# Layer 0's output product in one rounded pass over 96 rows, with GpSimd making a third of its operand

## The chip, the cores and the metric

The kernel runs on one core of a Trainium2 chip. The metric is device time in microseconds (us), the median of several runs. A core has five instruction streams that work beside each other and meet only through semaphores and DMA: TensorE (PE in the profile; its weight loads are PEld), VectorE (DVE), ScalarE (ACT), GpSimd (POOL) and SyncE (SP), which here only issues DMAs. Each executes its own list strictly in order.

## What is computed

128 entries of 64 rows, 256 wide, pass four conditioned residual layers, `x = x + layer(x)`:

```
# layer 0: a decoded low-rank map, K = 30
U = (mu @ W_dec + b_dec).reshape(B, 257, 30)
param = einsum('bik,kj->bij', U, V);  weight, bias = param[:, :-1], param[:, -1]
x = x + einsum('bsd,bde->bse', x, weight) + bias
# layer 1: demodulated linear map, clamped
y = einsum('blc,oc->blo', x * style, weight1) * dcoef
x = x + clip(y + bias1, -256, 256)
# layer 2: conditional adapter
x = x + relu(x @ (down*dg + db)) @ (up*ug + ub)
# layer 3: layer norms with gains looked up by class, then an MLP
h = ln(ln(x, pw_g[id], pw_b[id]), cp_g[c], cp_b[c]);  t = ln(x, tm_g[c], tm_b[c]);  s = ln(x, ms_g[m], ms_b[m])
x = x + ln(silu(cat([w0*h, w1*t, w2*(x+..), w3*(x+..), w4*(x+..), w5*s]) @ W1 + b1) @ W2 + b2, g, b)
```

Layer 0 is computed as t = U·x plus a bias part, 30 wide, and then x1 = x + t·V. The change is about t and t·V.

## The kernel before

The 8192 rows are 16 chunks of 512 rows, that is 8 entries each. Within a chunk TensorE does: t (L906: one bias product over 6 rows at L913, then 32 small u products at L919), x1 = t·V (L924, products at L935), l1 (layer 1, L948), dn and up (layer 2's adapter, L962 and L976), x3r and xht (transposes, L988 and L994), tm and ms (class gains of the t and s branches, L1008 and L1031), cp (class gains of h, L1035, products at L1046), hht (transposes of h, L994), and int_W1 in four parts whose names end in x3, tm, ms and h. int_W1 has its numbers split into high and low parts of the rounded float type fp32r, so each product is three, at L902, L903 and L904, of 128 rows by 512 columns.

x1's route through the engines is this. TensorE leaves t in PSUM in four strips of 32 rows. ScalarE's `act_th1` (th1, L1171) copies the four into rows 0 to 29 of `t_st`; its `act_th2` (th2, L1178) copies those to rows 32 to 61. `pe_x1` makes two fp32 products, one for each half of the features, each over its own 30 rows of `v_rep` and `t_st`. VectorE's `v_x1add` (L1345) adds x. GpSimd's `g_style` (style, L1516) multiplies by the style, and then l1 may run. So one chain goes th1, th2, x1, x1add, style, l1.

GpSimd also has, per chunk, hmul and hadd (L1546, L1551: h = xhat * gain + offset), wup (L1565, L1567: the adapter's weights), res (L1577), the gathers of table rows (L1507), and three small roots: rootx and rooth (L1523 to L1531, for the layer norms of x and h; their last result is nb_x or nb_h), and rooty (L1590, L1592, for the output's norm). rooty waits for ScalarE's squares y_sq (L1320) and is waited for by VectorE's y_out (L1486). ScalarE's normalisations of x and h stand at L1209 and wait for nb_x and nb_h.

The order of each queue is written out by hand as three lists (`run_slots`, L109): `begin`, then `order`, a list of (stage, lag) that a hardware loop repeats for iterations 6 to 15 (the stage works on chunk iteration minus lag), then `end`. So the steady part is ten iterations, and whatever stands ahead of iteration 6 or behind iteration 15 was placed by hand. Fillings (`pe_warm`, L537) are products of ones whose results nothing reads. `pads` is a list of tiles that are set to zero at the start, each element one more count of the semaphore `z_pad`.

Begin's setup part, up to the first chunk's x1, decodes U on TensorE (L487, 16 groups), builds tables and scales, and loads weights through SyncE's queue.

Of the kernel before, what the change touches and what calls it, by code (L numbers as in the profile page):

```python
# [122 lines left out]
def conditioned_residuals(nc, t):  # L123
    ctx = ExitStack()
    with ctx:
# [1683 lines left out]
```

## Time and profile before

| | us |
|---|---|
| runs (3) | 520.67, 521.92, 523.74; median 521.92 |
| profiled execution | 521.21 |
| its span on the chip | 519.4 |
| outside the span | 1.8 |

The profile is of one execution. Its page gives each engine's busy time, the busy share in 40 slices of the span, the chain that ended last, and groups of instructions by line. The trace behind it can be asked for single instructions: start, duration, the engine and line, tiles and shapes, and in brackets how long the engine stood idle before and what released it. Matmul ends are modelled and overlap, so the pace of TensorE is read from the starts. The mean granted TensorE clock was 0.994 of full speed.

### The profile page before, as it was taken

To read this page: it belongs to the slowest core of one execution; us is meant where nothing else is said; L and a number is where in the kernel's file an instruction comes from. 1 tells how busy PE (TensorE), PEld (TensorE's weight loads), DVE (VectorE), ACT (ScalarE), POOL (GpSimd) and SP (SyncE) were. 2 spreads that over 40 slices of the span, in tenths; PEclk is the share of its full clock that TensorE was granted. 3 is DMA by queue.
4 is the path that set the end of the run, shared out by engine and by line. 5 is a ranking of instruction groups with operands and counts; after the bars stand their busy time and mean duration, and the time that the engine had idled before them with its cause. 6 is when DMAs were issued, how large, how long until landed. Compare 5 with 4: busy or idle time off the path is not lost.

```text
span 519.4 us, 9425 instructions
## 1 busy us (share of the span) xinstructions
PE 486.3 (94%) x3198; PEld 354.2 (68%) x3198; DVE 405.8 (78%) x696; ACT 336.3 (65%) x638; POOL 391.0 (75%) x367
## 2 busy tenths in 40 slices
PE   2987887999999999999999999999999999998993
PEld 2953644767677776768686867677776768687682
DVE  2958876868788788888787878788787888886863
ACT  4573667456767676766777776767676767656832
POOL 6468799889878879697978787788779793787321
PEclk9999999999999999999999999999999999999997
DMA  8887705625252352608080716253442613104102
GB/s 299 247 304 208 203 20 124 163 73 135 83 127 81 77 171 56 191 24 223 0 229 17 205 43 173 74 136 112 106 142 63 175 47 90 49 21 145 40 2 81
DMA packets 34989, 61.78 MB, mean 119 GB/s; under 512 B 5017, under 2 KB 17413, under 8 KB 34580
## 3 DMA queue, kind: packets, MB, share of 16 engines
q1 hardware_dynamic: 28756, 43.98, 30.2%
q0 software_dynamic: 5344, 16.87, 11.3%
q10 hardware_dynamic: 864, 0.61, 0.4%
q8 instruction: 14, 0.23, 0.2%
q14 instruction: 11, 0.09, 0.1%
HBM read 52.58 MB, written 8.87 MB: 118 GB/s over the span
## 4 chain that ended last, share of the span: by engine, by line
PE 79%; POOL 6%; DVE 5%; DMA 4%; issue 3%; ACT 2%; SPq 0%; DVEq 0%; POOLq 0%; ACTq 0%
PE ps_c L902 11%; PE ps_c L904 11%; PE ps_c L903 10%; PE ps_d L948 9%; PE ps_d L962 5%; PE ps_a L976 5%; PE ps_b L902 3%; PE ps_b L903 3%; PE ps_b L904 3%; PE ps_b L935 2%; PE ps_a L988 2%; DMA set_wdec<-in_nets_rows 2%; PE ps_a L994 2%; PE ps_b L994 2%; DMA set_wdec<-in_W_dec 1%
## 5 line engine op out<-in xcount | busy, mean ns | idle before, releaser
L1507 POOL DMA_INDIRECT pw_rows<-in_pw,gidx x64 | 65.0, 1016 | 17.9 <-issue 17.4
L948 PE MATMUL ps_d<-xm_t,l_w 128*128 128x512 f32 x128 | 59.0, 603 | 2.2 <-POOL xm_t L1516 2.2
L1209 ACT ACTIVATE h<-h,nb_h,rstd_h 128x256 f32<-128x256 f32 x64 | 33.3, 591 | 33.1 <-POOL nb_h L1531 33.0
L1240 ACT ACTIVATE tm_t_h<-ps_a 128x1024 fp32r<-128x1024 f32 x16 | 16.4, 1026 | 45.6 <-DVE ps_a L1413 45.6
L1516 POOL TENSOR_TENSOR xm_t<-x_t,style 128x1024 f32<-128x1024 f32 x16 | 30.5, 1905 | 20.2 <-DVE x_t L1345 20.1
L948 PEld LDWEIGHTS ps_d<-xm_t,l_w 128*128 128x128 f32 x128 | 23.1, 190 | 26.8 <-issue 24.2
L1546 POOL TENSOR_TENSOR h<-xhat,pw_rows 128x1024 f32<-128x1024 f32 x16 | 38.0, 2378 | 4.1 <-ACT xhat L1209 4.1
L1565 POOL TENSOR_TENSOR w_up<-up_rep,ugub 128x1024 f32<-128x1024 f32 x16 | 38.0, 2372 | 2.2 <-issue 2.0
L1551 POOL TENSOR_TENSOR h<-h,pw_rows 128x1024 f32<-128x1024 f32 x16 | 38.3, 2394 | 1.3
L1567 POOL TENSOR_TENSOR w_up<-w_up,ugub 128x1024 f32<-128x1024 f32 x16 | 38.1, 2382 | 1.3
L902 PE MATMUL ps_b<-w_h,act_t_l 128*128 128x256 f32 x128 | 37.7, 294 | 0.4 <-DVE act_t_l L1450 0.4
L1577 POOL TENSOR_TENSOR x3be<-x,ln_gb 128x1024 f32<-128x1024 f32 x16 | 37.8, 2364 | 0.0
L1352 DVE TENSOR_TENSOR ps_d<-ps_d,dcoef 128x1024 f32<-128x1024 f32 x16 | 19.7, 1232 | 21.6 <-PE ps_d L948 21.6
L903 PE MATMUL ps_b<-w_l,act_t_h 128*128 128x256 f32 x128 | 36.1, 282 | 0.0
L904 PE MATMUL ps_b<-w_h,act_t_h 128*128 128x256 f32 x128 | 36.0, 281 | 0.0
L1209 ACT ACTIVATE xhat<-ps_a,nb_x,rstd_x 128x256 f32<-128x256 f32 x64 | 31.0, 564 | 6.7 <-POOL nb_x L1531 6.7
L962 PE MATMUL ps_d<-x_t,down_w 128*64 128x256 f32 x256 | 31.2, 385 | 3.0 <-DVE x_t L1367 3.0
L976 PEld LDWEIGHTS ps_a<-act_dn,w_up 128*128 128x128 f32 x256 | 30.5, 191 | 4.9 <-issue 2.6
L976 PE MATMUL ps_a<-act_dn,w_up 128*128 128x128 f32 x256 | 31.6, 277 | 2.2 <-ACT act_dn L1188 1.2
L1590 POOL TENSOR_TENSOR ve_y<-y_var,eps 128x4 f32<-128x4 f32 x15 | 3.0, 202 | 40.2 <-ACT y_sq L1320 40.2
L1418 DVE TENSOR_TENSOR ps_d<-ps_d,xh_t 128x1024 f32<-128x1024 f32 x16 | 19.7, 1231 | 17.4 <-PE ps_d L1031 17.4
L1320 ACT ACTIVATE y_sq<-ps_b 128x256 bf16<-128x256 f32 x64 | 23.7, 380 | 14.8 <-PE ps_b L904 14.8
(251 smaller groups left out, 1551.2 us busy)
## 6 DMA issues: line engine op xcount, KB each, us to landing
ugub<-ugub_scratch SPq DMA_DIRECT2D x32, 512.0 KB, 6.8
x_t<-in_x_t SPq DMA_DIRECT2D x16, 512.0 KB, 5.7
out<-y_out SPq DMA_DIRECT2D x15, 512.0 KB, 7.3
set_wdec<-in_W_dec SPq DMA_DIRECT2D x2, 1920.0 KB, 9.6
set_wdec<-in_int_W SPq DMA_DIRECT2D x1, 1536.0 KB, 9.8
set_wdec<-in_nets_rows SPq DMA_DIRECT2D x1, 1152.0 KB, 12.2
pw_rows<-in_pw,gidx POOLq DMA_INDIRECT x64, 3.7
set_wdec<-in_nets_W SPq DMA_DIRECT2D x1, 768.0 KB, 4.8
```

Source lines behind the costliest of these rows:

```text
L902: eng.matmul(out, wl, ah, start=first, stop=False)
L903: eng.matmul(out, wh, al, start=False, stop=False)
L904: return eng.matmul(out, wh, ah, start=False, stop=last)
L948: m = eng.matmul(ps_l1[:, o, :], l1_w[:, k, o * P:(o + 1) * P], xm_t[:, k, :], start=k == 0, stop=k == KB - 1)
L962: m = eng.matmul(ps_dn[e * HID:(e + 1) * HID, part * CT * S:(part + 1) * CT * S], down_w[:, k, part * HID:(part + 1) * HID], x[:, k, e], s ...
L976: m = eng.matmul(ps_up[:, k, j * P:(j + 1) * P], w_up[:, j, k * P:(k + 1) * P], act_dn[:, j, :, :], start=True, stop=True)
L1209: m = eng.activation(out[:, j, :], src[:, j, :], ACT.Identity, bias=nb[k][:, j:j + 1], scale=rstd[k][:, j:j + 1])
L1507: eng.indirect_dma_start(pw_rows[c.ring][:, j, :], None, t["pw"], bass.IndirectOffsetOnAxis(ap=gidx[c.ring][:, j:j + 1], axis=0)).then_inc ...
L1546: eng.tensor_tensor(h1[:, :, :], xhat[:, :, :], pw_rows[c.ring][:, :, 0:D], ALU.mult).then_inc(g_h1m, 1)
L1551: eng.tensor_tensor(h1[:, :, :], h1[:, :, :], pw_rows[c.ring][:, :, D:2 * D], ALU.add).then_inc(g_h1, 1)
L1565: eng.tensor_tensor(w_up[:, :, :], q, ugub[:, :, 0:D], ALU.mult).then_inc(g_upm, 1)
L1567: eng.tensor_tensor(w_up[:, :, :], w_up[:, :, :], ugub[:, :, D:2 * D], ALU.add).then_inc(g_up, 1)
```

## The change

- **x1 as one rounded product.** `t_st` becomes an fp32r tile of 96 rows: t's low part in rows 0 to 29, its high part in rows 32 to 61 and again in rows 64 to 93. `v_st`, made once, holds V's high part, its high part again, and its low part. x1 is then two products (one per half of the features) over all 96 rows.
- **t's route.** th1 writes t to an fp32 tile `t_f`, and waits for the low part of the chunk before. th2 copies `t_f` three times into `t_st` (three strips of 30 rows) and waits for x1 of the chunk before. A new stage on GpSimd, `g_tlow` (tlow, L1549 in the new file), writes t_f minus its high part into rows 0 to 29; it waits for th2. x1 waits for both. The two ScalarE semaphores become one that counts twice.
- **v_st.** `act_vhigh` on ScalarE (it waits for three weight loads, `up_rep` the last) and `v_vlow` on VectorE, once, in begin.
- **t's bias in strips.** One product of 6 rows by 128 columns becomes four of 128 rows by 32 columns; `ub_ch` and `entry_oh` are zeroed first.
- **cp in full rows.** The four cp products (24 rows each, in two row groups that ran in pairs) contract over all 128 rows; the gain table's unused rows are zeroed first.
- **Fillings.** `ones` is set first on GpSimd, and 22 products of ones stand ahead of the decoder. Six each follow x1(2), cp(0) and l1(2).
- **Tiles.** The class indices move to partitions 32 to 55 of the tile whose first rows are `t_f`.

```diff
-            wait(eng, a_th, c.n + 1)
+            if first(c):
+                eng.wait_ge(c_v, 2)
+            wait(eng, a_th, 2 * c.n + 2)
+            wait(eng, g_tl, c.n + 1)
             for k in range(KB):
-                rows = slice(k * RP, k * RP + RK)
-                m = eng.matmul(ps_x1[:, k, :], v_rep[rows, k * P:(k + 1) * P], t_st[rows, :], start=True, stop=True)
+                m = eng.matmul(ps_x1[:, k, :], v_st[:, k * P:(k + 1) * P], t_st[:, :], start=True, stop=True)
...
         def act_th1(eng, c):
             wait(eng, p_t, c.n + 1)
-            wait(eng, p_x1, c.n)
+            wait(eng, g_tl, c.n)
...
         def act_th2(eng, c):
-            wait(eng, a_th1, c.n + 1)
-            eng.activation(t_st[RP:RP + RK, :], t_st[0:RK, :], ACT.Copy).then_inc(a_th, 1)
+            if first(c):
+                eng.wait_ge(z_pad, len(pads))
+            wait(eng, a_th, 2 * c.n + 1)
+            wait(eng, p_x1, c.n)
+            for lo in (0, RP, 2 * RP):
+                m = eng.activation(t_st[lo:lo + RK, :], t_f, ACT.Copy)
+            m.then_inc(a_th, 1)
...
+        def g_tlow(eng, c):
+            wait(eng, a_th, 2 * c.n + 2)
+            low = t_st[0:RK, :]
+            eng.tensor_tensor(low, t_f, low.bitcast(F32), ALU.subtract).then_inc(g_tl, 1)
...
+        def act_vhigh(eng, c):
+            eng.wait_ge(d_wts, 48)
+            eng.activation(v_st[:, :], v_rep[:, :], ACT.Copy).then_inc(c_v, 1)
...
-            eng.matmul(ps_t[:, 0:2 * S], ub_ch[c.ring][0:2 * PIECES, :], entry_oh[0:2 * PIECES, :], start=True, stop=False)
+            for j in range(4):
+                strip = slice(j * RP, (j + 1) * RP)
+                eng.matmul(ps_t[strip, 0:2 * S], ub_ch[c.ring][:, strip], entry_oh[:, :], start=True, stop=False)
...
-            for j in (0, 2, 1, 3):
-                rows = slice(j // 2 * STRIP, j // 2 * STRIP + CLS)
-                m = eng.matmul(out[:, j, :], onehot[c.ring][rows, j * P:(j + 1) * P], gain_tab[rows, 0:D],
-                               start=True, stop=True)
+            for j in range(CT):
+                m = eng.matmul(out[:, j, :], onehot[c.ring][:, j * P:(j + 1) * P], gain_tab[:, 0:D], start=True, stop=True)
...
+        WARM = ((z_pool, 1, ps_b, 0, 22), (c_ug, 1, ps_d, 0, 13), (v_dca, 1, ps_a, 0, 13), (v_x1, 2, ps_b, 0, 7),
+                (v_x1, 2, ps_b, 0, 13), (v_row, 1, ps_c, 0, 6), (v_cls, 1, ps_c, 1, 6), (v_row, 1, ps_c, 0, 6))
...
-                      order=[(g_wup, 3), (g_hmul, 4), (g_hadd, 4), (g_rooty, 6), (g_gather, 2), (g_rooth, 4),
+                      order=[(g_wup, 3), (g_hmul, 4), (g_hadd, 4), (g_tlow, 2), (g_rooty, 6), (g_gather, 2), (g_rooth, 4),
```

Where tlow stands in GpSimd's queue is written out in its three lists, and ScalarE's order is as before. In the loop tlow stands between hadd and rooty, as the last line shows, in its first iteration for chunk 4. In begin it stands at four places. GpSimd in begin, around chunk 0's hmul and hadd, before (xhat and h are tiles of layer 3, pw_rows the gathered rows, w_up the adapter's weights):

```order
L1577 TENSOR_TENSOR x3be<-x,ln_gb 128x1024
L1546 TENSOR_TENSOR h<-xhat,pw_rows 128x1024
L1551 TENSOR_TENSOR h<-h,pw_rows 128x1024
L1565 TENSOR_TENSOR w_up<-up_rep,ugub 128x1024
L1567 TENSOR_TENSOR w_up<-w_up,ugub 128x1024
```

and after (idx_t is the tile that holds t_f):

```order
L1609 TENSOR_TENSOR x3be<-x,ln_gb 128x1024
L1578 TENSOR_TENSOR h<-xhat,pw_rows 128x1024
L1549 TENSOR_TENSOR t_st<-idx_t,t_st 30x512
L1583 TENSOR_TENSOR h<-h,pw_rows 128x1024
L1597 TENSOR_TENSOR w_up<-up_rep,ugub 128x1024
L1599 TENSOR_TENSOR w_up<-w_up,ugub 128x1024
```

So tlow(2) stands between hmul(0) and hadd(0). A little later in begin, GpSimd after rootx(1), before:

```order
L1526 TENSOR_TENSOR rstd_x<-ve_x,mhalf 128x4
L1531 TENSOR_TENSOR nb_x<-nm_x,rstd_x 128x4
L1565 TENSOR_TENSOR w_up<-up_rep,ugub 128x1024
L1567 TENSOR_TENSOR w_up<-w_up,ugub 128x1024
L1546 TENSOR_TENSOR h<-xhat,pw_rows 128x1024
```

and after:

```order
L1558 TENSOR_TENSOR rstd_x<-ve_x,mhalf 128x4
L1563 TENSOR_TENSOR nb_x<-nm_x,rstd_x 128x4
L1549 TENSOR_TENSOR t_st<-idx_t,t_st 30x512
L1597 TENSOR_TENSOR w_up<-up_rep,ugub 128x1024
L1599 TENSOR_TENSOR w_up<-w_up,ugub 128x1024
L1578 TENSOR_TENSOR h<-xhat,pw_rows 128x1024
```

So tlow(3) stands between rootx(1) and wup(2). In end, GpSimd between hadd(13) and rooty(11), before:

```order
L1546 TENSOR_TENSOR h<-xhat,pw_rows 128x1024
L1551 TENSOR_TENSOR h<-h,pw_rows 128x1024
L1590 TENSOR_TENSOR ve_y<-y_var,eps 128x4
L1592 TENSOR_TENSOR rstd_y<-ve_y,mhalf 128x4
L1523 TENSOR_TENSOR nm_h<-mv_h,mone 128x4
```

and after:

```order
L1578 TENSOR_TENSOR h<-xhat,pw_rows 128x1024
L1583 TENSOR_TENSOR h<-h,pw_rows 128x1024
L1549 TENSOR_TENSOR t_st<-idx_t,t_st 30x512
L1622 TENSOR_TENSOR ve_y<-y_var,eps 128x4
L1624 TENSOR_TENSOR rstd_y<-ve_y,mhalf 128x4
L1555 TENSOR_TENSOR nm_h<-mv_h,mone 128x4
```

So tlow(15) stands ahead of rooty(11), and rooth(13) comes behind both.

## Rows read from the trace of the kernel before

**Rows 1.** The page's first part: busy us, share of the span, instructions.

```profile
PE 486.3 (94%) x3198; PEld 354.2 (68%) x3198; DVE 405.8 (78%) x696; ACT 336.3 (65%) x638; POOL 391.0 (75%) x367
```

**Rows 2.** Waits, 130 to 410 us: waiter <- releaser: us in total, times, longest.

```profile
ACT tm_t_h L1240 <- DVE ps_a L1413: 34.8, 10, 4.6
...
POOL ve_y L1590 <- ACT y_sq L1320: 21.5, 10, 2.4
```

**Rows 3.** Timeline, TensorE, steady: start, us, engine, line, tiles, shapes, count.

```profile
271.81 0.39 PE L904 MATMUL ps_c<-ms_t_h,w_h 128*128 128x512 f32 x1
...
273.66 0.39 PE L903 MATMUL ps_c<-h_t_l,w_h 128*128 128x512 f32 x1
...
277.18 0.22 PE L913 MATMUL ps_b<-entry_oh,ub_ch 6*128 6x128 bf16 x1
...
277.92 3.70 PE L948 MATMUL ps_d<-xm_t,l_w 128*128 128x512 f32 x8
```

**Rows 4.** Groups by line and shape: busy us, mean ns of one, idle before.

```profile
L1178 ACT ACTIVATE t_st<-t_st 30x512 f32<-30x512 f32 x16 | 10.1, 630 | 0.4
...
L537 PE MATMUL ps_d<-ones 128*128 128x512 bf16 x13 | 3.0, 380 | 0.0
L836 POOL TENSOR_TENSOR w_l<-set_w1x,w_h 128x512 fp32r<-128x512 f32 x1 | 1.3, 1271 | 0.0
```

**Rows 5.** Timeline of the setup, TensorE (decoder) and SyncE's queue (weights).

```profile
9.47 2.04 PE L487 MATMUL ps_a<-set_mu,set_w_rt 128*128 128x128 f32 x8 [9.47 <-ACT set_w_rt L696]
...
15.96 1.95 PE L487 MATMUL ps_d<-set_mu,set_w_rt 128*128 128x128 f32 x16
...
23.58 0.46 SPq L439 DMA_DIRECT2D up_rep<-in_up_p  x1
```

**Rows 6.** Timeline, GpSimd, at tlow(2) and tlow(3).

```profile
69.50 2.37 POOL L1551 TENSOR_TENSOR h<-h,pw_rows 128x1024 f32<-128x1024 f32 x1
...
76.58 1.18 POOL L1523 TENSOR_TENSOR nm_h<-mv_h,mone 128x4 f32<-128x4 f32 x1
...
86.64 2.34 POOL L1565 TENSOR_TENSOR w_up<-up_rep,ugub 128x1024 f32<-128x1024 f32 x1
...
102.50 1.02 POOL L1523 TENSOR_TENSOR nm_h<-mv_h,mone 128x4 f32<-128x4 f32 x1 [1.29 <-DVE mv_h L1403]
...
108.29 1.91 POOL L1516 TENSOR_TENSOR xm_t<-x_t,style 128x1024 f32<-128x1024 f32 x1 [0.89 <-DVE x_t L1345]
```

**Rows 7.** Timeline, ScalarE: th2 of chunks 2, 4 and 15, and the normalisation ahead of th2(3).

```profile
70.00 0.63 ACT L1178 ACTIVATE t_st<-t_st 30x512 f32<-30x512 f32 x1
...
86.72 1.94 ACT L1209 ACTIVATE xhat<-ps_a,nb_x,rstd_x 128x256 f32<-128x256 f32 x4 [0.30 <-POOL nb_x L1531]
...
129.25 0.63 ACT L1178 ACTIVATE t_st<-t_st 30x512 f32<-30x512 f32 x1
...
435.90 0.63 ACT L1178 ACTIVATE t_st<-t_st 30x512 f32<-30x512 f32 x1
```

**Rows 8.** Timeline, TensorE: tm(1), l1(4) and l1(15).

```profile
118.96 0.39 PE L1008 MATMUL ps_a<-onehot,gain_tab 24*128 24x512 bf16 x2 [0.24 <-ACT xhat L1209]
...
138.99 3.70 PE L948 MATMUL ps_d<-xm_t,l_w 128*128 128x512 f32 x8
...
443.86 3.60 PE L948 MATMUL ps_d<-xm_t,l_w 128*128 128x512 f32 x8
```

**Rows 9.** Timeline, GpSimd, first iteration (rooty(0), style(4)), and a steady rooty.

```profile
126.62 0.21 POOL L1590 TENSOR_TENSOR ve_y<-y_var,eps 128x4 f32<-128x4 f32 x1
...
136.13 1.91 POOL L1516 TENSOR_TENSOR xm_t<-x_t,style 128x1024 f32<-128x1024 f32 x1 [1.29 <-DVE x_t L1345]
...
293.08 0.20 POOL L1590 TENSOR_TENSOR ve_y<-y_var,eps 128x4 f32<-128x4 f32 x1 [1.89 <-ACT y_sq L1320]
```

**Rows 10.** Timeline of the end: GpSimd's rooty(11) and style(15), VectorE's y_out(11).

```profile
432.04 0.20 POOL L1590 TENSOR_TENSOR ve_y<-y_var,eps 128x4 f32<-128x4 f32 x1 [2.29 <-ACT y_sq L1320]
...
441.72 1.91 POOL L1516 TENSOR_TENSOR xm_t<-x_t,style 128x1024 f32<-128x1024 f32 x1 [6.01 <-DVE x_t L1345]
...
436.13 1.66 DVE L1486 SCALAR_TENSOR_TENSOR y_out<-ps_b,rstd_y,x3be 128x256 f32<-128x256 f32 x4
```

More of the change, by code:

```diff
@@ L183, in conditioned_residuals @@
         act_dn = sb("act_dn", [P, CT, 2, S])
-        t_st = sb("t_st", [2 * RP, CH])
+        t_st = sb("t_st", [PIECES * RP, CH], F32R)
         x_t = [sb(f"x_t{r}", [P, KB, CH]) for r in range(2)]
@@ L188, in conditioned_residuals @@
         ugub = sb("ugub", [P, CT, 2 * D])
-        idx_ch = [sb(f"idx_ch{r}", [CLS, CH], I32) for r in range(2)]
+        idx_t = [sb(f"idx_t{r}", [2 * RP, CH]) for r in range(2)]
+        idx_ch = [tile[RP:RP + CLS, :].bitcast(I32) for tile in idx_t]
+        t_f = idx_t[0][0:RK, :]
         gidx = [sb(f"gidx{r}", [P, CT], I32) for r in range(2)]
@@ L281, in conditioned_residuals @@
             sem("m_" + n) for n in "tail dec st ug dc hid mo mot row cls".split())
-        c_rt, c_exp, c_style, c_dg, c_ug, c_sqr, c_hid, c_mot, c_w1, c_w2h, c_shift = (
-            sem("c_" + n) for n in "rt exp style dg ug sqr hid mot w1 w2h shift".split())
+        c_rt, c_exp, c_style, c_dg, c_ug, c_sqr, c_hid, c_mot, c_w1, c_w2h, c_shift, c_v = (
+            sem("c_" + n) for n in "rt exp style dg ug sqr hid mot w1 w2h shift v".split())
         (z_pad, v_ub, v_rt, v_dec, v_soft, v_sq, v_dca, v_mo, v_row, v_cls, v_pick,
@@ L531, in pe_warm @@
         def pe_warm(eng, c):
-            s, v, out, count = ((c_ug, 1, ps_d[:, 0, :], 13), (v_dca, 1, ps_a[:, 0, :], 13),
-                                (v_x1, 2, ps_b[:, 0, :], 7), (v_x1, 2, ps_b[:, 0, :], 13))[c.n]
-            eng.wait_ge(z_pool, 5)
+            s, v, ps, k, count = WARM[c.n]
+            eng.wait_ge(z_pool, 1)
             eng.wait_ge(s, v)
             for _ in range(count):
-                eng.matmul(out, ones[:, :], ones[:, :].unsqueeze(1).broadcast_to([P, CH // P, P]), start=True, stop=True)
+                eng.matmul(ps[:, k, :], ones[:, :], ones[:, :].unsqueeze(1).broadcast_to([P, CH // P, P]), start=True, stop=True)
         def pe_mot(eng, c):
@@ L779, in act_shift, with g_ones @@
             m.then_inc(c_shift, 1)
+        def g_ones(eng, c):
+            eng.memset(ones[:, :], 1.0).then_inc(z_pool, 1)
         def g_init(eng, c):
@@ L1052, in pe_hht @@
             newest(eng, c, (v_x1, 2), (v_y, -2))
-            newest(eng, c, (a_th1, 3), (v_x1, 2), (v_y, -2))
+            newest(eng, c, (v_x1, 2), (v_y, -2))
+            if ahead(c, 3):
+                wait(eng, a_th, 2 * (c.n + 3) + 1)
             wait(eng, v_h, c.n + 1)
@@ L1167, in act_th1 @@
             wait(eng, p_t, c.n + 1)
-            wait(eng, p_x1, c.n)
-            out = t_st[0:RK, :].rearrange("r (q j s) -> r q j s", j=4, s=S)
+            wait(eng, g_tl, c.n)
+            out = t_f.rearrange("r (q j s) -> r q j s", j=4, s=S)
             for j in range(4):
@@ L1331, in act_onehot @@
             wait(eng, s_idx[c.ring], 32 * (c.half + 1))
-            eng.activation(oh_sq[:, :], idx_ch[c.ring][:, :], ACT.Square, bias=cls_neg[:, 0:1]).then_inc(a_sq, 1)
+            eng.activation(oh_sq[:, :], idx_ch[c.ring][:, :], ACT.Square, bias=cls_neg[RP:RP + CLS, 0:1]).then_inc(a_sq, 1)
             wait(eng, a_sq, c.n + 1)
```

69 lines of the change are left out of this document (37 added, 32 removed).

## The prediction

> **What bounds the kernel now.** I read the page's first part, then the waits of the loop, then the timelines at the places that the change touches. TensorE is busy 94% of the span, GpSimd 75%, VectorE 78%, ScalarE 65% [rows 1]. In the loop (ten iterations) the longest waits are those of the other engines: ScalarE waits 34.8 us ahead of tm_t_h, 3.5 per iteration, and GpSimd 21.5 us ahead of rooty, 2.15 per iteration [rows 2]. So in the steady part only TensorE's own work counts, and there is room on ScalarE and GpSimd. In begin and end that isn't so: there l1 and tm start right behind what GpSimd and ScalarE hand over. tm(1) waited 0.24 us for the normalisation of x [rows 8], and l1(4), at 138.99, started 0.95 us after style(4) had ended (136.13 + 1.91) [rows 8, 9].
>
> **The steady part: TensorE's saving.** The eight products (four cp, four x1) stand between the last ms product at 271.81 and the h products, of which the second starts at 273.66 [rows 3]. Two ordinary products of 512 columns lie in that stretch, at the pace of (273.66 - 271.81 being 1.85) 0.23 us each; so cp and x1 cost 1.85 - 0.46 = 1.39 us. After, x1 is two fp32r products of 512 columns like their neighbours, 0.46 us, and cp four bf16 products over 256 columns. The nearest row is 13 bf16 products of 512 columns in 3.0 us of busy time with their overlaps, about 0.22 each [rows 4], so 0.11 for 256 columns and 0.43 for four. With about 0.1 for changing over that is 1.0: a saving of 0.4 per chunk (between 0.3, if the fp32r pair starts late, and 0.5). t's bias now needs four products of 32 columns; t with its bias takes 0.74 us now, from 277.18 to 277.92 [rows 3]. The one product is only 0.15 to 0.2 of that, the four can't be more than 0.1 away from it either way, and I take 0.
>
> What row and rule say about full rows: the cp products ran as pairs in two row groups, and the change gives that up. The Trainium skill ("TensorEngine Tiling (Array Packing)", When to Use Tiling) advises row tiling for contractions of up to 64 rows, which speaks against this change, while its Key Properties say that changing the tiling mode drains TensorE, which speaks for it. By the first alone cp would cost twice what it does; by the trace's own pace above the sum of cp and x1 still falls, so it changes no term.
>
> **The steady part: the added work.** th2's two more copies are 2 x 0.63 = 1.26 us on ScalarE per chunk [rows 4]; its wait of 3.5 per iteration takes them. tlow, 30 x 512 in fp32, is not in the trace. The nearest row is the same operation on 128 x 512, 1.27 us [rows 4]; above, a 128 x 1024 one takes 1.91 [rows 6]; below, nothing excludes 0.64, as for th2's copy of this shape. I take 1.27 by the column count. In the loop tlow stands ahead of rooty, where GpSimd waits 2.15 per iteration (1.89 at 293.08 [rows 9]), so it costs nothing there. That cover has only 0.6 us to spare. So the loop should save 0.4 per chunk. With chunks 3, 4 and 15 inside the stalls below, ten count: 10 x 0.4 = **-4.0** (between -3 and -5.5).
>
> **The setup.** The first eight decoder products take 2.04 us at 9.47, sixteen later ones 1.95 [rows 5]. The filling ahead of the decoder (22 x about 0.22 = 4.8 us, up to two times that at the lower clock, in a stretch where TensorE has nothing to do until 9.47) would bring the first groups to the later pace, about 2 us over the first groups. Less of that reaches the first chunk: act_vhigh, ahead of u(0) on ScalarE, waits for up_rep, which SyncE issues at 23.58 [rows 5] and which still has to land, and the first chunk gets th2's 1.26 and tlow's 1.27 on the way to its style, each less what it overlaps. Behind vhigh on ScalarE stand u(0), the exponential, ug, th1, th2 and the root for dcoef. I take **+0.3** net, between -1.5 and +2.5.
>
> **Begin, stall A: tlow(2).** It stands between hmul(0) and hadd(0). Before, hadd(0) starts at 69.50 [rows 6]. tlow(2) waits for th2(2), whose single copy starts at 70.00 [rows 7]; three copies end at 70.0 + 3 x 0.63 = 71.9, and tlow at 71.9 + 1.27 = 73.2. hadd(0) then is 3.65 late.
>
> **Stall B: tlow(3).** It stands ahead of wup(2), before at 86.64 [rows 6]. th2(3) comes on ScalarE behind the normalisation of x(1), 86.72 to 88.66 [rows 7], so its three copies end at 90.6 and tlow at 91.9: +5.25. This normalisation itself waits for GpSimd's nb_x(1), so it is late by A already, and the two add. With about 0.6 of fillings (18 products in all, mostly in TensorE's own gaps) hadd(1) is 9.5 late. Behind it, rooth(1) at 102.50 had waited 1.29 and style(3) at 108.29 had waited 0.89 for VectorE [rows 6]; these waits go first: 9.5 - 1.3 - 0.9 = **+7.4** at tm(1), by rootx(2), the normalisation of x(2) and its 0.24 [rows 8].
>
> **Stall C: tlow(4),** at the loop's entry. ScalarE's th2(4) starts only at 129.25 [rows 7], behind work of chunks 0 to 2. Three copies end at 131.15, tlow at 132.4; rooty(0) stood at 126.62 [rows 9], so +5.8. What is queued behind it on GpSimd: the gathers, rooth(2), style(4). style(4) had waited 1.29 [rows 9], so it is 4.5 late and ends at 142.6 (138.04 + 4.5), against l1(4) at 138.99 [rows 8]: **+3.6**.
>
> **Stall D: tlow(15),** in end, ahead of rooty(11). th2(15) starts at 435.90 [rows 7], three copies end at 437.8, tlow at 439.1; rooty(11) stood at 432.04 [rows 10]: +7.1. VectorE's y_out(11), at 436.13, waits for rooty's result, which then comes at 439.1 + 1.25 = 440.35: +4.2. Behind y_out stand x1add(15), style(15) at 441.72 [rows 10] and l1(15) at 443.86 [rows 8]. style(15) ended 0.23 before that, so **+4.0**.
>
> **The sum.** 0.3 + 7.4 + 3.6 + 4.0 - 4.0 = +11.3 us on the profiled execution's 521.2: 532.5. The median of the runs lies 0.7 above that execution; the forecast for the median is **533 us**. About 0.5% is what a measurement of this kernel can tell from no change: 519.3 to 524.5.
>
> **Rivals.**
> 1. *Not slower: the stalls are paid from slack.* If GpSimd arrived late anyway at the four places (its queue in begin is later by the setup's changes, ScalarE's th2 earlier), tlow would find its data ready and cost 1.27 each, which the waits of 0.9 to 1.3 behind it take. Then 13 chunks save 0.4 each: 521.9 - 5.2, about **516.5**. For it: A is only 2.4 us of waiting (69.50 to 71.9). Against it: three of the four are 4 us or more. It needs GpSimd later by over 4 us, or th2 earlier. Chance 0.10.
> 2. *Half of the stalls.* TensorE in begin has gaps of its own, and I read only the chain that I followed. If two of the four are covered, A with B counting 3.7 or C with D halved, the sum is near 3 to 4: **525** (523 to 529). Chance 0.17.
> 3. *GpSimd bounds the loop.* tlow eats 1.27 of a wait of 1.89. If it took over 1.9 us, each chunk would cost what lies above. There is a row for such a thing: nm_h at 76.58 took 1.18 us where it usually takes 0.20, beside a VectorE subtraction of two SBUF tiles [rows 6]. Up to 1.2 more on 1.27 is 2.5, 0.6 over the wait, 10 x 0.6 = +6 and the stalls longer by as much: **540**. In the loop VectorE's such operations stand behind y_out, which waits for the rooty behind tlow, so they don't meet. The point from which it decides is tlow at 1.9 us. Chance 0.04. The Trainium skill ("SBUF — State Buffer", section "SBUF: two separate sides") tells of an exclusive lock on a port pair shared by VectorE and GpSimd, taken by VectorE operations with two SBUF inputs; the row at 76.58 agrees with it. By that rule a tlow beside such an operation would wait for its whole length, which is this rival.
> 4. *The change doesn't do what it says.* If the fp32r pair over 96 rows and cp in full rows are no cheaper (1.39 as before), the -4.0 is gone: **537**. Against it: the products around them are fp32r and run at 0.23 each [rows 3]. Chance 0.04.
>
> **Chances and range.** The forecast's own case, three or four stalls paid in full, has 0.65; its range is 528 to 538 by the saving (1.5 either way), the setup (-1.8, +2.2) and tlow between 0.64 and 1.9 (four times 0.6, -2.5 and +2.5). The rivals 0.10, 0.17, 0.04 and 0.04. The range for 8 in 10 reaches down into rival 2 and up to rival 4: 524 to 538. Faster by over 0.5%: rival 1 and a little of rival 2, 0.12. Within 0.5%: the lower part of rival 2, 0.08. Slower: 0.80.
>
> **What would show it.** In the profile after: ScalarE's th2 as 48 copies of about 0.63; tlow, sixteen, of about 1.27, with idle time of GpSimd ahead of it in four places, about 2.4, 4.0, 4.5 (131.15 - 126.67) and 5.8 to 8 us, released by ScalarE's t_st, and none in the loop. x1's two products at TensorE's pace of 0.23 and cp's at 0.11; the loop's period down by 0.4. TensorE idle ahead of l1(3) or tm(1), of l1(4) and of l1(15), by 7, 3.6 and 4 us. I am wrong if tlow is over 1.9 us, if the period doesn't fall, or if one of the four waits is there but TensorE isn't idle behind it; the last would mean that another engine's slack, which I did not follow, took it.

## The result

The changed kernel takes **535.4 us** (median of four runs, 534.7 to 538.3) against 522.2 of before: a ratio of 1.026, with a 95% interval of 1.022 to 1.031. It is slower, as forecast. The profiled execution took 535.4 with a span of 533.6, which is 14.2 more than before's; the prediction's sum had 11.3.

The page of the changed kernel, engines and granted clock:

```profile
PE 492.7 (92%) x3225; PEld 366.3 (69%) x3254; DVE 406.0 (76%) x701; ACT 356.6 (67%) x671; POOL 408.6 (77%) x383
...
PEclk9989898998989999999999999999999999999998
```

TensorE's share fell from 94% [rows 1] to 92%: it now waits. The second line is TensorE's granted clock in tenths: five of the 40 slices in the first part are below nine tenths, and the last one. Before, only the last slice was:

```profile
PEclk9999999999999999999999999999999999999997
```

The two added operations, from the groups by line and shape, answering to [rows 4]:

```profile
L1203 ACT ACTIVATE t_st<-idx_t 30x512 fp32r<-30x512 f32 x48 | 30.0, 625 | 0.5
L1549 POOL TENSOR_TENSOR t_st<-idx_t,t_st 30x512 fp32r<-30x512 f32 x16 | 20.2, 1265 | 21.2 <-ACT t_st L1203 21.2
```

th2's copies take 0.63 us each and tlow 1.265, as taken from the rows of before. GpSimd stood idle for 21.2 us ahead of tlow. The four places, from GpSimd's timeline of the changed kernel:

```profile
74.02 1.26 POOL L1549 TENSOR_TENSOR t_st<-idx_t,t_st 30x512 fp32r<-30x512 f32 x1 [2.44 <-ACT t_st L1203]
...
98.61 1.26 POOL L1549 TENSOR_TENSOR t_st<-idx_t,t_st 30x512 fp32r<-30x512 f32 x1 [3.82 <-ACT t_st L1203]
...
142.03 1.29 POOL L1549 TENSOR_TENSOR t_st<-idx_t,t_st 30x512 fp32r<-30x512 f32 x1 [4.91 <-ACT t_st L1203]
...
448.11 1.27 POOL L1549 TENSOR_TENSOR t_st<-idx_t,t_st 30x512 fp32r<-30x512 f32 x1 [8.16 <-ACT t_st L1203]
```

These are tlow(2), tlow(3), tlow(4) and tlow(15): 2.4, 3.8, 4.9 and 8.2 us, where the prediction had 2.4, 4.0, 4.5 and 5.8 to 8. The fifth wait is chunk 0's, 1.9 us.

What TensorE did behind them, from its timeline (in brackets its idle time and what ended it; "issue" at up(1) is the wait for w_up, which wup(1) writes behind tlow(2) and hadd(0), until 83.19):

```profile
83.29 3.37 PE L997 MATMUL ps_a<-act_dn,w_up 128*128 128x128 f32 x16 [5.26 <-issue]
...
120.77 5.10 PE L969 MATMUL ps_d<-xm_t,l_w 128*128 128x512 f32 x8 [2.47 <-POOL xm_t L1542]
...
146.79 0.71 PE L956 MATMUL ps_b<-t_st,v_st 96*128 96x512 f32 x2 [2.05 <-DVE y_out L1512]
...
154.90 3.67 PE L969 MATMUL ps_d<-xm_t,l_w 128*128 128x512 f32 x8 [1.56 <-DVE h L1454]
...
452.49 0.71 PE L956 MATMUL ps_b<-t_st,v_st 96*128 96x512 f32 x2 [3.01 <-DVE y_out L1512]
...
458.37 3.67 PE L969 MATMUL ps_d<-xm_t,l_w 128*128 128x512 f32 x8 [1.50 <-POOL xm_t L1542]
```

These are up(1), l1(3), x1(4), l1(4), x1(15) and l1(15).

The steady part, TensorE, answering to [rows 3]: the last ms product, cp and x1, the second h product; then t's bias in strips and l1.

```profile
285.43 0.39 PE L921 MATMUL ps_c<-ms_t_h,w_h 128*128 128x512 f32 x1
285.65 0.61 PE L1066 MATMUL ps_d<-gain_tab,onehot 128*128 128x256 bf16 x4
286.02 0.72 PE L956 MATMUL ps_b<-t_st,v_st 96*128 96x512 f32 x2
...
286.82 0.39 PE L920 MATMUL ps_c<-h_t_l,w_h 128*128 128x512 f32 x1
...
290.34 0.24 PE L932 MATMUL ps_b<-entry_oh,ub_ch 128*32 128x128 bf16 x4
...
290.95 3.70 PE L969 MATMUL ps_d<-xm_t,l_w 128*128 128x512 f32 x8
```

cp and x1 cost 286.82 - 285.43 - 0.46 = 0.93 us, against 1.39: 0.46 less. t with its bias takes 0.61, against 0.74: 0.13 less. So the loop should save 0.59 per chunk, and from tm(2) to tm(12) it saved 0.58 each.

A ledger by the starts of TensorE's stages, each less the start of the same stage in before (us). The three right columns are experiments told below.

| start of | changed | e1_retimed | e5_gapfill | e12_only_c |
|---|---|---|---|---|
| l1(1) | +2.2 | +2.0 | -0.7 | +1.4 |
| l1(2) | +7.8 | +3.3 | +0.6 | +8.7 |
| tm(1) | +11.0 | +2.7 | +0.1 | +12.1 |
| l1(4) | +15.9 | +3.2 | +0.5 | +12.4 |
| tm(12) | +10.1 | -2.6 | -5.3 | +6.5 |
| l1(15) | +14.5 | -2.7 | -5.4 | +11.0 |
| span | +14.2 | -3.0 | -5.7 | +10.7 |

### The profile page after: what moved, and what is told of

It is laid out like the page before. It is cut to its first block, busy times and chain, and to the rows that moved or that the text cites. A ratio compares the mean times of both kernels' runs of the same rounds, so it can differ in the third digit from the quotient of the medians.

```text
span 533.6 us, 9664 instructions
## 1 busy us (share of the span) xinstructions
PE 492.7 (92%) x3225; PEld 366.3 (69%) x3254; DVE 406.0 (76%) x701; ACT 356.6 (67%) x671; POOL 408.6 (77%) x383
## 4 chain that ended last, share of the span: by engine, by line
PE 63%; POOL 13%; issue 9%; DVE 6%; ACT 4%; DMA 4%; SPq 0%; ACTq 0%; POOLq 0%; DVEq 0%
PE ps_c L919 8%; PE ps_c L921 8%; PE ps_c L920 8%; PE ps_d L969 8%; PE ps_a L997 5%; PE ps_d L983 4%; POOL pw_rows L1533 3%; PE ps_b L919 3%; PE ps_b L920 2%; PE ps_b L921 2%; PE ps_a L1009 2%; PE ps_b L1015 2%; PE ps_a L1015 2%; DMA set_wdec<-in_W_dec 1%; POOL h L1583 1%
## 5 line engine op out<-in xcount | busy, mean ns | idle before, releaser
L969 PE MATMUL ps_d<-xm_t,l_w 128*128 128x512 f32 x128 | 60.3, 615 | 5.5 <-POOL xm_t L1542 4.0
L997 PE MATMUL ps_a<-act_dn,w_up 128*128 128x128 f32 x256 | 34.5, 293 | 6.5 <-issue 5.3
L997 PEld LDWEIGHTS ps_a<-act_dn,w_up 128*128 128x128 f32 x256 | 33.3, 207 | 9.1 <-issue 8.3
L1266 ACT ACTIVATE tm_t_h<-ps_a 128x1024 fp32r<-128x1024 f32 x16 | 16.4, 1027 | 30.3 <-DVE ps_a L1439 30.3
L1549 POOL TENSOR_TENSOR t_st<-idx_t,t_st 30x512 fp32r<-30x512 f32 x16 | 20.2, 1265 | 21.2 <-ACT t_st L1203 21.2
L1512 DVE SCALAR_TENSOR_TENSOR y_out<-ps_b,rstd_y,x3be 128x256 f32<-128x256 f32 x64 | 26.5, 477 | 8.8 <-POOL rstd_y L1624 5.4
```

The costliest lines, as they stand in the source:

```text
L969: m = eng.matmul(ps_l1[:, o, :], l1_w[:, k, o * P:(o + 1) * P], xm_t[:, k, :], start=k == 0, stop=k == KB - 1)
L997: m = eng.matmul(ps_up[:, k, j * P:(j + 1) * P], w_up[:, j, k * P:(k + 1) * P], act_dn[:, j, :, :], start=True, stop=True)
```

## Experiments

Theory, called *place*: GpSimd's queue waits at four places for ScalarE's th2, what stands behind it comes late, and TensorE has no slack there. Rivals: *work* (the added copies and subtractions lengthen begin and end wherever they stand), and *clock*, which the page brought up (the fillings and dense products let the granted clock fall, and that is the loss).

**e1_retimed.** The four waits taken away by order alone:

```diff
-  (g_hmul, 0), (g_tlow, 2), (g_hadd, 0), (g_wup, 1)
+  (g_hmul, 0), (g_hadd, 0), (g_tlow, 2), (g_wup, 1)
-  (g_rootx, 1), (g_tlow, 3), (g_wup, 2) ... (g_gather, 2), (g_rooth, 1)
+  (g_rootx, 1), (g_wup, 2) ... (g_gather, 2), (g_tlow, 3), (g_rooth, 1)
-  (act_xnorm, 2), (act_tmh, 1) ... (act_x3h, 2), (act_th2, 4)
+  (act_xnorm, 2), (act_th2, 4), (act_tmh, 1) ... (act_x3h, 2)
-  (act_hh, 12), (act_tmh, 12) ... (act_onehot, 13), (act_th2, 15)
+  (act_hh, 12), (act_th2, 15), (act_tmh, 12) ... (act_onehot, 13)
```

> The changed kernel with its four waiting places retimed and nothing else: on GpSimd tlow(2) behind hadd(0) and tlow(3) behind the gathers of chunk 2 (ahead of rooth(1)); on ScalarE th2(4) behind the normalisation of x(2) and th2(15) behind the copy of h(12)'s high part. Theory 'place' (GpSimd waiting for th2 is the loss): A and B some 9 us, C 4.9 and D 4.5 go, the loop's saving of 5.8 stays: 535.4 - 18 = about 517, faster than before. Rival 'work' (the added copies and subtractions themselves lengthen begin and end, wherever they stand): over 530. Rival 'clock' (fillings and wide products let the TensorE clock fall, whatever the stalls): half-clock stretches remain and the time is about 522 to 525.

Measured: 517.7 us, ratio to before 0.989 (0.985 to 0.992), so faster than before. *Place* is right within 1 us and *work* falls: the same work in other places is 17 us shorter (spans 533.6 and 516.4). The ledger shows what remained: 3.2 us in begin. Of the four places only tlow(4)'s was also taken away alone (next); the parts of A with B and of D are read from the ledger.

**e12_only_c.** The changed kernel with the third pair of lines above alone.

> The changed kernel with th2(4) alone moved on ScalarE (behind the normalisation of x(2)); the waits of tlow(2), tlow(3) and tlow(15) stay. The prediction put 3.6 us on tlow(4); by the changed kernel's trace l1(4) is 4.9 later than tm(1), of which a half-clock stretch at 148 us, behind TensorE's idle time of 2.0 there, may be a part. If the stalls add up as the prediction has it: l1(4) 3.6 to 4.9 earlier than in the changed kernel, the stretch at 148 gone, and the difference stays to the end: ratio to before 1.017 to 1.020. If other engines' lateness from tlow(2) and tlow(3) covers it: no change, 1.026.

Measured: 530.9 us, ratio 1.013 (1.008 to 1.018), somewhat lower than the 1.017 to 1.020 expected. tlow(4) no longer waits. l1(4) is 3.5 earlier than in the changed kernel, at the lower edge of what was expected, and 3.5 stays to the end; the clock is full from 146 to 152 us. From tm(1) to l1(4) it is 0.3, where the changed kernel lost 4.9; 1.1 of that difference is tm(1)'s own, which was that much later in this execution. So C's stall comes on top of the others and isn't covered by them, as the prediction had it.

**e2_nofill** and **e3_nofill0.** The changed kernel without all of the added fillings, and without the 22 ahead of the decoder alone:

```diff
-  begin=[(pe_warm, 0), (pe_dec, 0)
+  begin=[(pe_dec, 0)
-  (pe_x1, 2), (pe_warm, 5), (pe_x3r, 1), (pe_cp, 0), (pe_warm, 6), (pe_t, 3), (pe_l1, 2), (pe_warm, 7)
+  (pe_x1, 2), (pe_x3r, 1), (pe_cp, 0), (pe_t, 3), (pe_l1, 2)
```

(e3_nofill0 has the first pair only.)

> The changed kernel without its four added fillings (the 22 ahead of the decoder and the three of six). Theory 'the stalls bring the half-clock stretches' (TensorE idle, then full work): the stretches at 35, 55, 82, 120 and 148 us stay, only the first, at 11 us, goes; time within 1.5 of 535.4. Rival 'the fillings bring them': clock back to 0.99, and the time 3 to 6 us lower, 530 to 532.

> The changed kernel without the 22 fillings ahead of the decoder alone. If these bring the stretches at half clock in the setup (11, 35, 55 us): they go or move, the setup is 1 us longer by the decoder's slower first groups, time 533 to 536. If the stalls bring them: all but the first stay, time 535 to 537.

Measured: e2_nofill 537.4, ratio 1.026 (1.022 to 1.030); e3_nofill0 538.6, ratio 1.028 (1.023 to 1.032). On this chip before took 523.4, so both are as slow as the changed kernel. In e2_nofill the stretches with a clock below full are at 36, 57, 84, 121 and 149 us, as in the changed kernel but for the first, and one more is at 452 us, behind tlow(15)'s wait. In e3_nofill0 they are at 34, 81, 122, 157 and 457 us: that at 55 is gone, against what was expected, and that at 148 came behind the next wait. *Clock* falls as far as it blames the fillings.

**e4_before_fill.** The kernel before with the added fillings alone, and `ones` set first on GpSimd for them:

```diff
-            eng.wait_ge(z_pool, 5)
+            eng.wait_ge(z_pool, 1)
...
+  WARM = ((z_pool, 1, ps_b, 0, 22), ... (v_row, 1, ps_c, 0, 6), (v_cls, 1, ps_c, 1, 6), (v_row, 1, ps_c, 0, 6))
-  begin=[(pe_dec, 0), ...
+  begin=[(pe_warm, 0), (pe_dec, 0), ...
```

> The kernel before with only the added fillings (ones set first, 22 ahead of the decoder, three times six in begin). Prediction's view (fillings lie in gaps and start the decoder faster): 521.5, within 1. Rival 'fillings bring half-clock stretches': granted clock 0.98, 523 to 526.

Measured: 523.9 us, ratio 1.002 (0.999 to 1.006): no change that can be told. Its profiled execution shows why nothing came of the faster decoder. style(0) and l1(0) are 2.0 us earlier than in before, as the prediction had it for the decoder, and then VectorE waits for a weight transfer. Its row in before, and in e4_before_fill:

```profile
40.92 0.97 DVE L629 TENSOR_TENSOR ps_c<-ps_c,set_wdec 128x768 f32<-128x768 f32 x1 [4.51 <-DMA set_wdec<-in_nets_rows]
```

```profile
42.91 0.97 DVE L631 TENSOR_TENSOR ps_c<-ps_c,set_wdec 128x768 f32<-128x768 f32 x1 [8.51 <-DMA set_wdec<-in_nets_rows]
```

The transfer was issued 2.3 us earlier (25.95 against 28.22), beside others that were still under way, and took 16.4 us in place of 12.2. VectorE's l1mul(0) and x2add(0) stand behind it, so TensorE waited 4.9 us ahead of dn(0) and l1(1) was 2.6 late. dn(0) then ran at half clock, 3.61 us in place of 1.95. This stretch, behind a wait, is the only one ahead of the end in this execution, although all the fillings are there.

**e5_gapfill.** e1_retimed with the setup's fillings laid into TensorE's idle times:

```diff
-  WARM = ((z_pool, 1, ps_b, 0, 22), (c_ug, 1, ps_d, 0, 13), ...
+  WARM = ((z_pool, 1, ps_b, 0, 28), (c_ug, 1, ps_d, 0, 4), ..., (c_ug, 1, ps_d, 0, 9))
-  (pe_hid, 0), (pe_x1, 0), (pe_warm, 1), (pe_mo, 0)
+  (pe_hid, 0), (pe_warm, 8), (pe_x1, 0), (pe_warm, 1), (pe_mo, 0)
```

> e1_retimed with the fillings laid into the idle times of TensorE of over 2 us in the setup: 28 ahead of the decoder in place of 22, and of the 13 behind x1(0) nine ahead of it. In e1_retimed TensorE stood idle from 7.5 to 9.4 and from 31.9 to 34.1 us, and each was followed by a stretch at half clock (from 11 and 35 us), a third came at 55 us. Theory 'a stretch at half clock follows idle time of 2 us': the stretches at 11 and 35 go, l1(0) is up to 1 us earlier, total 516 to 518. Rival 'they follow the dense work': the stretches stay, and total is the same or 1 us longer.

Measured: 516.6 us, ratio 0.991 (0.987 to 0.995), which doesn't differ from e1_retimed's 0.989. The profiled execution was the fastest of ten; its span is 513.7, 2.7 below e1_retimed, and all of it gained before l1(1). Windows of six us, first of the changed kernel and then of e5_gapfill (the seventh entry is the granted clock):

```profile
34.00:40.00 6.00, 5.79 (x19) 2.74 (x20) 2.83 (x2) 5.96 (x14) 3.48 (x6) 0.72 1.03 349
54.00:60.00 6.00, 4.79 (x23) 4.06 (x23) 4.59 (x8) 5.60 (x9) 5.06 (x5) 0.72 0.95 231
82.00:88.00 6.00, 4.71 (x23) 3.94 (x24) 1.22 (x1) 3.03 (x6) 5.19 (x7) 0.72 0.58 130
120.00:126.00 6.00, 5.23 (x11) 2.47 (x12) 2.62 (x9) 2.70 (x6) 4.86 (x7) 0.72 0.45 117
146.00:152.00 6.00, 5.21 (x17) 4.17 (x18) 4.02 (x5) 0.54 (x2) 5.12 (x8) 0.72 0.63 178
```

```profile
34.00:40.00 6.00, 4.17 (x18) 2.51 (x16) 2.94 (x3) 5.99 (x13) 3.91 (x5) 1.00 0.85 308
54.00:60.00 6.00, 5.96 (x38) 4.08 (x39) 4.87 (x5) 5.74 (x8) 5.07 (x5) 1.00 0.97 255
```

**e11_after_gapfill.** The changed kernel, its waits kept, with the same edit of the fillings.

> The changed kernel, its four waiting places kept, with the setup's fillings laid out as in e5_gapfill. Tells what part of its excess over the prediction was the half clock of the setup: if 'a stretch follows idle time of 2 us', the stretches before 60 us go and those behind the waits of tlow(2), tlow(3) and tlow(4) stay (at 82, 120 and 148 us), and the time is 2 to 3 us below the changed kernel's, near 533. If it stays at 535, the setup's clock did not matter.

Measured: 537.1, ratio 1.024 (1.018 to 1.029), which the intervals can't tell from the changed kernel's. The stretches at 11 and 35 us are gone; l1(0) is only 0.1 us later than in before, where it was 1.6 later in the changed kernel. But the stretch at 53 to 59 us is there and longer than in the changed kernel, so l1(1) is 1.9 late again. Those at 81, 121 and 149 us, behind the waits of tlow(2) to tlow(4), stayed, and one came at 452 us, behind tlow(15)'s wait. So the stretches behind the idle times that were filled went, but not the one at 55, and the gain didn't come.

**e6_pool**, **e10_both.** In e1_retimed up(1) still waited 2.1 us for w_up. e6_pool puts tlow(2) behind wup(1), and W2's low part behind style(2); e10_both adds e5_gapfill's edit.

```diff
-  (g_hadd, 0), (g_tlow, 2), (g_wup, 1), (g_rooth, 0), (g_w1xlow, 0), (g_w2low, 0), (g_style, 2), (g_w1mlow, 0)
+  (g_hadd, 0), (g_wup, 1), (g_tlow, 2), (g_rooth, 0), (g_w1xlow, 0), (g_style, 2), (g_w2low, 0), (g_w1mlow, 0)
```

> e1_retimed with tlow(2) one place later still on GpSimd, behind wup(1), and the low part of W2 behind style(2). In e1_retimed up(1) waited 2.1 us for wup(1), which tlow(2) had moved by 1.27. Theory 'a subtraction on GpSimd costs its 1.27 where GpSimd is what TensorE waits for': l1(2) is 1.2 earlier than in e1_retimed and stays so, 516.5. Rival 'begin is bound elsewhere': no change, 517.7.

> e5_gapfill and e6_pool together. In the profiled runs e5_gapfill was 2.7 us and e6_pool 0.7 us below e1_retimed, by different means (no half-clock stretch; up(1) earlier). If they add, with the tail's -5.7 of e5_gapfill: about 512.5 in its profile, and a median 9 us below before (ratio 0.983). If the second is inside the first: as e5_gapfill, ratio 0.989.

Measured: e6_pool 517.7, ratio 0.992 (0.989 to 0.995), e10_both 517.0 on a chip where before took 523.9, ratio 0.985 (0.981 to 0.990). l1(2) was 1.3 us earlier in e6_pool than in e1_retimed, of which 0.4 was there at l1(1) already, ahead of the edit; only 0.7 was left at the end of the profiled execution, and the median is the one that was expected for no change. In e10_both the clock fell again from 53 to 57 us; its span is 515.5, not the 512.5 expected if the two gains added. The ratios of e1_retimed, e5_gapfill, e6_pool and e10_both overlap: each is faster than before, by 0.8 to 1.5%, and which is best isn't settled.

**e8_strips_cp.** The kernel before with t's bias in strips and cp in full rows, x1 left as it was.

```diff
-            eng.matmul(ps_t[:, 0:2 * S], ub_ch[c.ring][0:2 * PIECES, :], entry_oh[0:2 * PIECES, :], start=True, stop=False)
+            for j in range(4):
+                strip = slice(j * RP, (j + 1) * RP)
+                eng.matmul(ps_t[strip, 0:2 * S], ub_ch[c.ring][:, strip], entry_oh[:, :], start=True, stop=False)
...
-            for j in (0, 2, 1, 3):
...
+            for j in range(CT):
...
```

(The cut lines are cp's products, over 24 rows in two row groups before and over all 128 here, as in the changed kernel, and the zeroing of the added rows.)

> The kernel before with only t's bias in strips and cp in full rows; x1 stays in fp32 over 30 rows. Prediction put 0 on the strips and 0.96 less 0.43 on cp and x1 together. By the changed kernel's trace, t is 0.13 shorter, and cp with x1 0.46. If the strips' part is theirs alone, the period falls by 0.13 from them; cp in full rows alone saves nothing or costs up to 0.2, since its row pairs are given up while x1 keeps its own: period 27.6 to 27.9 against 27.77, time within 2 us of before.

Measured: 523.1 us, ratio 1.004 (1.001 to 1.008), and a period of 27.98 us, 0.2 longer than before's and just above what was expected. TensorE in its steady part, first in before and then here:

```profile
272.13 0.28 PE L1046 MATMUL ps_d<-gain_tab,onehot 24*128 24x256 bf16 x2
272.15 0.69 PE L935 MATMUL ps_b<-t_st,v_rep 30*128 30x512 f32 x1
...
273.31 0.51 PE L902 MATMUL ps_c<-h_t_h,w_l 128*128 128x512 f32 x1
```

```profile
275.06 0.39 PE L905 MATMUL ps_c<-ms_t_h,w_h 128*128 128x512 f32 x1
275.30 0.61 PE L1048 MATMUL ps_d<-gain_tab,onehot 128*128 128x256 bf16 x4
275.84 1.13 PE L938 MATMUL ps_b<-t_st,v_rep 30*128 30x512 f32 x4
276.89 0.50 PE L903 MATMUL ps_c<-h_t_h,w_l 128*128 128x512 f32 x1
277.23 0.39 PE L904 MATMUL ps_c<-h_t_l,w_h 128*128 128x512 f32 x1
```

From the ms product to the second h product it is 2.17 us, against 1.85 in before: cp in full rows costs 0.32 while x1 stays in row groups. The strips save 0.12 here too. In before x1's first product starts 0.02 us behind cp's first pair, and the eight take 1.18 us (272.13 to 273.31); x1's four alone take 1.05 here (275.84 to 276.89). So cp's row pairs cost only some 0.13 beside x1. Of the changed kernel's 0.59, taken in this order, the strips are 0.13, cp's full rows -0.32, and x1 as one product behind them 0.78. In the other order the parts differ, as the next run shows.

**e9_cp_pairs.** e10_both with cp back in its row pairs, and x1 over 96 rows.

> e10_both with cp again as four products over 24 rows in two row groups; x1 stays one product over 96 rows. In e8_strips_cp cp in full rows beside x1 in row pairs lengthened cp and x1 together by 0.32 us per chunk. Theory 'full rows cost cp its pairing whatever x1 is': 0.1 to 0.3 us less per chunk, period 26.9 to 27.1, 2 to 4 us in all. Rival 'changing between row groups and full rows is what costs' (two changes more per chunk here than in e10_both): 0 to 0.3 more per chunk, up to 4 us longer.

Measured: 517.5 us, ratio 0.987 (0.983 to 0.991), the same as e10_both; but the loop saves 0.50 per chunk and not 0.57. That is 0.07, where four executions with cp in full rows lie within 0.02 of each other. It goes the rival's way: with x1 in full rows, pairs are slightly the dearer form. The rows show both sides: cp's first product starts 0.32 us behind the last ms product (0.23 in full rows), and from cp to x1 it is 0.32 (0.37 in full rows). So cp's row pairs were nearly free in before, beside x1's row groups, and once x1 has left these, cp is no worse off in full rows. The Trainium skill ("TensorEngine Tiling (Array Packing)", When to Use Tiling) advises row groups for contractions this short; in these runs that pays only where the neighbours use them too. The Trainium skill says on the same page, under Key Properties, that changing the mode drains TensorE, which fits the 0.09 us ahead of cp's first product; no run shows the drain apart from the rest.

**e7_twice.** e1_retimed with the subtraction made twice, the first into a tile that nothing reads:

```diff
+            if first(c):
+                eng.wait_ge(c_v, 2)
+            eng.tensor_tensor(v_rep[0:RK, :].bitcast(BF16), t_f, low.bitcast(F32), ALU.subtract)
             eng.tensor_tensor(low, t_f, low.bitcast(F32), ALU.subtract).then_inc(g_tl, 1)
```

> e1_retimed with the subtraction of tlow made twice (the first result goes to a tile that nothing reads), so tlow is 2.5 us and not 1.27. Prediction's rival 3: GpSimd's wait ahead of rooty, 0.55 per iteration in e1_retimed, is the whole cover, so each iteration is longer by 1.27 - 0.55 = 0.7, ten of them 7, and begin and end by 1 to 4: 526 to 529. If GpSimd has more slack than this wait shows (its other wait ahead of style, 1.1 per iteration, gives way too): under 521.

Measured: 535.1 us (two runs), ratio 1.026 (1.019 to 1.032), above what was expected. The loop's chunks became 0.88 us longer than in e1_retimed (0.7 expected), and begin 8.5 longer up to l1(4) (1 to 4 expected). Its waits from 130 to 410 us have one of TensorE's that before doesn't have:

```profile
PE ps_d L969 <- DVE h L1454: 9.8, 10, 2.3
```

TensorE waits for VectorE's product of h, which waits for ScalarE's normalisation, which waits for GpSimd's root. So with 1.26 us more GpSimd bounds the loop, as the third rival said, and by somewhat more than its wait ahead of rooty would leave. From what length of tlow on it does wasn't tried. How little is left with one tlow, from the waits of the changed kernel over the same stretch, answering to [rows 2]:

```profile
ACT tm_t_h L1266 <- DVE ps_a L1439: 19.0, 10, 2.6
...
POOL ve_y L1622 <- ACT y_sq L1346: 5.1, 9, 0.7
```

2.15 us per iteration have become some 0.55.

## Why the prediction was right, and where it was off

The forecast was 533 us within 524 to 538, slower with a chance of 0.80; it came to 535.4. Step by step, against the ledger:

- **The steady part's saving.** Forecast 0.4 per chunk, measured 0.58. The total is -5.8 against -4.0. Two terms were mis-sized: the strips, taken at 0, save 0.13, and cp with x1 cost 0.93 where 1.0 was taken, of which 0.1 was for changing over. In the rows of the changed kernel the first cp product starts 0.22 us behind the last ms product, which is the ordinary pace (in before it was 0.32, 271.81 to 272.13), so that 0.1 isn't there.
- **The added work in the loop.** Right: 0.63 per copy, 1.265 for tlow, no wait ahead of tlow in the loop, and the cover ahead of rooty down to 0.55, where 0.6 was forecast.
- **The setup.** Forecast +0.3, measured +2.2 at l1(1). This is the step that failed by most. The decoder's later groups did start 0.8 us sooner, and style(0) was 0.9 later. But TensorE then stood idle for 2.1 us ahead of x1(0), and the 13 fillings behind it ran at half clock, 4.67 us in place of 2.98; up(0), at 55 us, ran at half clock as well, 3.65 in place of 2.02. In the profiled execution of e5_gapfill, where the clock was full, l1(1) is at -0.7. e11_after_gapfill, where only the stretches at 11 and 35 are gone, has l1(0) at +0.1 and l1(1) at +1.9. The prediction had no term for the clock, since no row of before shows it below full ahead of the last slice.
- **A and B, tlow(2) and tlow(3).** Forecast +7.4 at tm(1), measured 11.0 - 2.2 = 8.8. The waits were right (2.4, and 3.8 for 4.0). A reached TensorE not by the h chain alone but by w_up: TensorE stood 5.3 us ahead of up(1), which the prediction didn't follow. Between hadd(0), +5.8, and the normalisation of x(1), +8.1, 2.3 us came on top where 0.6 for fillings had been taken. The rows show two parts of it: GpSimd's addition in wup(1) took 3.20 us in place of 2.35, beside a VectorE subtraction (last section), and up(1) ran at half clock, 3.37 us in place of 2.05. At tm(1) itself TensorE didn't wait. It had waited 2.5 ahead of l1(3) for style(3), and l1(3) then ran at half clock, 5.10 in place of 3.70. So what set tm(1) was style(3) with l1(3). The path that the prediction followed, by rootx(2) and the normalisation of x(2), came out nearly as late: that normalisation ended 0.3 us ahead of tm(1).
- **C, tlow(4).** Forecast +3.6, measured +4.9 in the changed kernel, and 3.5 at the end by e12_only_c. The path was another than told: GpSimd's rooty(0) was late, VectorE's y_out(0) with it, and x1(4) waited 2.0 for y_out; then the h products ran at 0.43 us each in place of 0.23 until 151 us, and l1(4) waited 1.6 for VectorE's h. style(4) was not the last to come. The prediction had rooty 5.8 late, and it was 5.7 later than tm(1) was; the way on from there was another than the one named, so that the size came out near is in part luck.
- **D, tlow(15).** Forecast +4.0, measured +4.4. y_out(11) was 4.5 late where 4.2 had been forecast. But TensorE waited 3.0 of it ahead of x1(15), for y_out itself, and only 1.5 ahead of l1(15), for style(15). The step from y_out to x1 was missing here too.
- **The sum.** 2.2 + 8.8 + 4.9 - 5.8 + 4.4 - 0.3 (end) = 14.2. The begin was mis-sized by 4.6, the loop by -1.8, D by 0.4 and the end by -0.3. That these partly cancel is luck, and it made the total better than its terms.
- **The rivals.** That the stalls are paid from slack didn't happen: e1_retimed shows the time without them, 517.7, near the 516.5 that this rival named for it. The second rival's sum doesn't come out: with A and B at 3.7 in place of 7.4, or with C and D halved, it is near 7.6 (529), and 3.8 (525) only with both. The third rival's 540 leaves next to nothing for the stalls, which its tlow of 2.5 us would have lengthened as well. That the new products are no cheaper is excluded by 0.93 against 1.39.

**The clock.** At half clock are some 3.4 us at each of six places in the changed kernel, from 11, 35, 55, 82, 120 and 148 us; none in before ahead of its end. The rows at the last one show it without a model:

```profile
147.35 0.45 PE L919 MATMUL ps_c<-h_t_h,w_l 128*128 128x512 f32 x1
147.59 0.63 PE L920 MATMUL ps_c<-h_t_l,w_h 128*128 128x512 f32 x1
148.02 0.63 PE L921 MATMUL ps_c<-h_t_h,w_h 128*128 128x512 f32 x1
...
150.99 0.39 PE L919 MATMUL ps_c<-h_t_h,w_l 128*128 128x512 f32 x1
```

Starts are 0.23 us apart, then 0.43, then 0.23 again: the two levels, 2.4 and 1.2 GHz. Ahead of five of the six TensorE had stood idle for 2.0 to 5.3 us, and where the idle time was taken away the stretch behind it went: those at 11 and 35 us in e5_gapfill and e11_after_gapfill, and that at 148 in e12_only_c. In e12_only_c that at 11 us is gone too, and there TensorE stood idle for 1.0 us ahead of the decoder, where it was 2.1 in the changed kernel. That much is shown. What isn't: when a stretch comes. Idle times of 2 to 3 us were not always followed by one (none behind 77.9 to 80.0 in e1_retimed; none behind the 3.0 ahead of x1(15) in the changed kernel, but one behind the same 3.0 in e2_nofill, e3_nofill0, e11_after_gapfill and e12_only_c). The stretch around 55 us, without such an idle time, came in some kernels and not in others whose idle times there were alike. The Trainium skill ("TensorE: Matmul & The Clock Gate", HAM oscillation) says that waits between bursts of products bring the clock down; the five places agree with it. How much of the 14.2 us is the clock's isn't separable by these runs, since waits and clock go together. What it costs at a place where TensorE sets the pace is 1.3 at up(1), 1.4 at l1(3), and 1.6 in the rows at 148 us (eight products 0.2 slower each).

## What to carry to other kernels

Each engine's queue runs in order, so an operation that waits for another engine holds up all that stands behind it. Put it where its input is already there, and look this up again in the hand-written begin and end, where the loop's lags don't hold: the order alone was worth 17 us here, while the cheaper products were worth 6. Count a stall on the engine that sets the pace as more than its length, since here the granted clock often fell behind it. Follow a late result along every way it has, also to the products that wait to write where it was read: x1 waited for y_out, and the prediction missed that twice. And before taking a product out of its row groups, look at what its neighbours use.

## What the runs showed of the hardware beyond the expected

- A transfer issued 2.3 us earlier landed 1.9 later, since it took 16.4 us in place of 12.2 beside others (e4_before_fill). In that execution the faster start of the decoder was worth nothing by that.
- In e1_retimed VectorE's subtraction of two SBUF tiles took 2.53 us, where it takes 1.22 to 1.30 elsewhere, beside GpSimd's addition on w_up that had begun earlier and ended at 79.90. First VectorE's row, then GpSimd's:

```profile
78.45 2.53 DVE L1463 TENSOR_TENSOR x_t_l<-x_t,x_t_h 128x1024 fp32r<-128x1024 f32 x1
```

```profile
77.55 2.35 POOL L1599 TENSOR_TENSOR w_up<-w_up,ugub 128x1024 f32<-128x1024 f32 x1
```

From 79.90, when GpSimd's operation ended, to 80.98 is 1.1 us, about VectorE's whole operation: it stood for the rest of GpSimd's. In before it began 0.2 us ahead of that end. The Trainium skill ("SBUF — State Buffer", Who interferes with whom) has this as a lock held for a whole instruction, and the rows agree.
- In the changed kernel the same two operations met the other way round, and GpSimd's, on which up(1) waited, was the one that paid: 3.20 us in place of 2.35. VectorE's row, then GpSimd's:

```profile
79.57 1.43 DVE L1463 TENSOR_TENSOR x_t_l<-x_t,x_t_h 128x1024 fp32r<-128x1024 f32 x1
```

```profile
79.99 3.20 POOL L1599 TENSOR_TENSOR w_up<-w_up,ugub 128x1024 f32<-128x1024 f32 x1
```

From 81.00, when VectorE's operation ended, to 83.19 is 2.2 us, about GpSimd's whole operation.
